# Where the denominators of the first four heads stand in TensorE's program

## The chip, the cores and the metric

The kernel runs on one core of a Trainium2 chip. The metric is the device time of one execution in microseconds, lower is better. In the profile PE is TensorE's matmuls, PEld its weight loads, DVE is VectorE, ACT is ScalarE, POOL is GpSimd and SP is SyncE.

## The reference

The input is 32 sequences of 256 tokens with 256 features. First come four recurrent (sLSTM) layers with their feed-forward parts, then, per sequence, an attention over a context and a quantised feed-forward layer. The change lies in the attention:

```python
q, k, v = (heads(q), heads(k), heads(v))          # 16 heads of 64 features
sim = jnp.einsum('bhid,bhjd->bhij', q, k) * SCALE
sim = jnp.where(mask[:, None, None, :], sim, max_neg)
sim = jnp.clip(sim, -5.0, 5.0)
attn = jax.nn.softmax(sim, axis=-1)
out = jnp.einsum('bhij,bhjd->bhid', attn, v)
```

Since the scores are clipped to -5 and 5, no maximum is taken off ahead of the exponential. The kernel multiplies the exponentials with the values, and separately with ones, which gives the denominators; the quotient is taken behind both.

## The kernel before, in words

The program has two stages, one after the other. The first holds the recurrent layers (lines up to 585). The second, `attend_and_feed` from line 586, has a loop over the batch of B = 32 sequences, written out by hand for each engine: each engine has its own queue in a fixed order, and semaphores tie them together. Batch j holds the projections and the attention of sequence j, woven with the feed-forward part of sequence j - 1 and the layer norms of sequence j + 2.

The attention of a batch goes in four quads q of four heads each. For quad q:

- `scores(j, pair)` on TensorE (line 857) forms the scores of two heads. It writes them to two of three PSUM banks (SCORES = 3), so a pair waits until VectorE has clipped the older heads in these banks: `clip_done` of 2 * pair - 1 heads.
- `clip(j, i)` on VectorE (line 1175) clips and masks the scores of head i into the SBUF tile `scores`, a ring of eight heads.
- `exps(j, i)` on ScalarE (line 1027) takes the exponential in place.
- `add_halves(j, i)` on POOL (line 771) adds the two halves (128 keys each) of the exponentials of head i, into the tile `exps_of_both_halves`. Behind the add of head 3 POOL splits the context of sequence j + 2 into a high and a low f16 part (`context_split`, lines 757 and 759), and behind the adds of heads 7, 11 and 15 it forms the low part of the attended values of the quad before (line 775).
- `attend(j, q, 0)` and `attend(j, q, 1)` on TensorE (line 867) multiply the exponentials of four heads with the first and the second half of their value features. The first waits for the exponentials of all four heads and for `ot_done`, the product of the quad before.
- `denominators(j, q)` on TensorE (line 879) multiplies the added halves of four heads with ones. It waits for `halves_added` of all four heads.
- `denominators(j, q)` on ScalarE (lines 1071 and 1073) takes the logarithm of the denominators, and the exponential of its negative. In ScalarE's order it stands between the exponentials of heads 4q + 5 and 4q + 6.
- `attended(j, q)` on VectorE (line 1260) multiplies the attended values with the inverse denominators.
- `out_project` on TensorE (line 911) projects the result.

VectorE's order around quad 0 of batch j, for 0 < j < 30: clips of heads 4 and 5; the rounding down of the first token tile of the hidden values (`h_round_down(f, 0)`, line 1231); clips of heads 6 and 7; `attended(j, 0)`; the rounding up of the second tile (`h_round_up(f, 1)`, line 1227, a multiplication and an addition over 128x1024 f32 from SBUF to SBUF); clips of heads 8 and 9; the low part of the next inputs (line 1322); the rounding down of the second tile (line 1231).

TensorE's order in a batch: the projections, and the first four score heads; then per quad what stands in the loop below. `x1_features` (line 902) turns the next batch's normed inputs, `transpose_h` and `feed_out` belong to the feed-forward part.

```python
for q in range(QUADS):
    if q + 1 < QUADS:
        scores(j, 2 * q + 2)
    if q == 0 and j + 1 < B:
        x1_features(j + 1)
    attend(j, q, 0)
    if q + 1 < QUADS:
        scores(j, 2 * q + 3)
    denominators(j, q)
    attend(j, q, 1)
```

Of the kernel before, what the change touches and what calls it, by code (L numbers as in the profile page):

```python
# [585 lines left out]
def attend_and_feed(nc, ctx, a, x4, out, kept):  # L586
# [128 lines left out]
    with nc.Block() as block:  # L715
# [91 lines left out]
        def _(pe):  # L807
# [39 lines left out]
            def scores(j, pair):  # L847

                if pair == 0:
                    pe.wait_ge(lo_done, SPLIT * (j + 1))  # L850
                else:
                    pe.wait_ge(clip_done, AHEADS * j + 2 * pair - 1)
                for kt in range(KT):
                    for part, (k_, q_) in enumerate(((k_hi, q_hi), (k_lo, q_hi), (k_hi, q_lo))):
                        for hh in range(2):
                            r = slice(ADH * hh, ADH * (hh + 1))
                            mm = nc.tensor.matmul(bank[:, (2 * pair + hh) % SCORES, kt * S:(kt + 1) * S],  # L857
                                                  k_[r, pair, kt * P:(kt + 1) * P], q_[r, pair, :], start=part == 0, stop=part == 2)
                            if kt == KT - 1 and part == 2:
                                mm.then_inc(s_ready, 1)  # L860

            def quad(j, q, stationary, b, at, done):

                for kt in range(KT):
                    for g in range(4):
                        i = 4 * q + g
                        mm = nc.tensor.matmul(bank[32 * g:32 * g + 32, b, at:at + S], stationary(kt, i),  # L867
                                              pr[:, i % RING, kt * S:(kt + 1) * S], start=kt == 0, stop=kt == KT - 1,
                                              skip_group_check=True)
                if done is not None:  # L870
                    mm.then_inc(done, 1)

            def denominators(j, q):
                n = QUADS * j + q
                pe.wait_ge(halves_added, 4 * (n + 1))
                if n > 0:
                    pe.wait_ge(den_step, 2 * n - 1)
                for g in range(4):
                    mm = nc.tensor.matmul(bank[32 * g:32 * g + 32, DEN, 0:S], ones32[:], psum[:, (4 * q + g) % RING, :], start=True,  # L879
                                          stop=True, skip_group_check=True)  # L880
                mm.then_inc(den_ready, 1)

            def attend(j, q, half):
                n = QUADS * j + q
                if half == 0:
                    pe.wait_ge(exp_done, 4 * (n + 1))
                    if q == 0:
                        pe.wait_ge(v_done, QUARTERS * (j + 1))
                    if n > 0:
                        pe.wait_ge(ot_done, n)  # L890
                quad(j, q, lambda kt, i: v[:, kt, i, 32 * half:32 * half + 32], AV, half * S, av_done if half else None)
# [4 lines left out]
            def x1_features(n):  # L896
                pe.wait_ge(x1_step, X1_OPS * (n + 1))
                if n > 1:
                    pe.wait_ge(h_done, ROUNDS * (n - 1))
                for h in range(HALF):  # L900
                    for tt in range(QT):
                        mm = nc.tensor.transpose(bank[:, FFB, h * S + tt * P:h * S + (tt + 1) * P], x1[:, tt, h * P:(h + 1) * P], identf[:])  # L902
                mm.then_inc(x1_turned, 1)
# [13 lines left out]
            def transpose_x(j, tt):  # L917
                pe.wait_ge(quant_step, x_quantised(j, tt))
                for h in range(HALF):
                    mm = nc.tensor.transpose(bank[:, OUTB, :].bitcast(BF16)[:, tt * D + h * P:tt * D + (h + 1) * P],  # L920
                                             xq[:, tt, h * P:(h + 1) * P], identb[:])
                mm.then_inc(xqt_ready, 1)

            def feed_in(j, r):

                tt, c = r // 2, r % 2
                if c == 0:
                    pe.wait_ge(xqt_done, QT * j + tt + 1)
                if r == 0 and j == 0:
                    pe.wait_ge(ff_ready, 1)  # L930
                if r == 0 and j > 0:
                    pe.wait_ge(z_done, QT * j)
                for m, read in enumerate((gate_done, h_done)):
                    if r > 0:
                        pe.wait_ge(read, ROUNDS * j + r)
                    w_ = ff_t[:, m, :].rearrange("p (h n) -> p h n", h=HALF)
                    for h in range(HALF):
                        mm = nc.tensor.matmul(bank[:, FFB + m, :], xqt[:, tt, h, :], w_[:, h, c * 512:(c + 1) * 512],  # L938
                                              start=h == 0, stop=h == HALF - 1)
                mm.then_inc(gu_ready, 1)  # L940

            def transpose_h(j):
                for tt in range(QT):
                    pe.wait_ge(hquant_step, h_quantised(j, tt))
                    if tt == 0 and j + 2 < B:
                        pe.wait_ge(x1_split, j + 3)
                    for c in range(FF // P):
                        mm = nc.tensor.transpose(bank[:, FFB + tt, :].bitcast(BF16)[:, c * P:(c + 1) * P],  # L948
                                                 hq[:, tt, c * P:(c + 1) * P], identb[:])
                    mm.then_inc(hqt_ready, 1)  # L950

            def feed_out(j):
                for tt in range(QT):
                    pe.wait_ge(hqt_done, QT * j + tt + 1)
                    w_ = ff_t[:, 2, :].rearrange("p (c n) -> p c n", c=FF // P)
                    for c in range(FF // P):
                        mm = nc.tensor.matmul(bank[:, FFB + tt, 0:D], hqt[:, tt, c, :], w_[:, c, :], start=c == 0,  # L957
                                              stop=c == FF // P - 1)
                    mm.then_inc(down_ready, 1)

            def first_units():
                for u in range(QUARTERS):
                    unit(0, u)
                for u in range(SPLIT, UNITS):
                    unit(0, u)
                pe.wait_ge(ident_ready, 2)
                x1_features(0)
                for u in range(QUARTERS, SPLIT):
                    unit(0, u)
                scores(0, 0)  # L970
                pe.wait_ge(ff_parts, 3)
                nc.tensor.matmul(bank[:, FFB + 1, 0:3], onesf[:], ff_part[:], start=True, stop=True).then_inc(ff_sums, 1)
                scores(0, 1)

            pe.wait_ge(consts, 1)
            for j in range(B):
                f = j - 1
                if j == 0:
                    first_units()
                else:  # L980
                    for u in range(UBANKS):
                        unit(j, u)
                    transpose_x(f, 0)
                    unit(j, UBANKS)
                    feed_in(f, 0)
                    transpose_x(f, 1)
                    for r in range(1, ROUNDS):
                        unit(j, UBANKS + r)
                        feed_in(f, r)
                    scores(j, 0)  # L990
                    unit(j, SPLIT + 1)
                    scores(j, 1)
                    unit(j, SPLIT + 2)
                    unit(j, SPLIT + 3)
# [3 lines that stand above are left out]
                    if q == 0 and j + 1 < B:  # L998
                        x1_features(j + 1)
                    attend(j, q, 0)  # L1000
                    if q + 1 < QUADS:
                        scores(j, 2 * q + 3)
                    denominators(j, q)
                    attend(j, q, 1)
                    if q == 2 and j > 0:
                        transpose_h(f)
                    if q == 3 and j > 0:
                        feed_out(f)
                    if q > 0:
                        out_project(j, 2 * q - 2)  # L1010
                        out_project(j, 2 * q - 1)
                out_project(j, APAIRS - 2)
                out_project(j, APAIRS - 1)
# [519 lines left out]
```

## Time and profile before

| what | value |
|---|---|
| median of 3 runs | 3733.89 us (3730.02 to 3734.52) |
| the profiled execution | 3732.63 us |
| its span | 3730.9 us |
| TensorE matmul busy | 3615.0 us, 97% |
| VectorE busy | 3460.5 us, 93% |
| ScalarE busy | 3064.7 us, 82% |
| GpSimd busy | 2253.7 us, 60% |
| granted TensorE clock, mean | 0.99 |
| batches of the second stage | from about 2262 us on |

The span is what the profiler saw between the first and the last instruction. A row of the timeline gives the start in microseconds from the span's start, the time taken, the engine, the line of the kernel, the instruction, what it writes and reads with its shape, and how many instructions the row merges; square brackets give the idle time of the engine ahead of it and who ended it. Matmuls are pipelined: a matmul's own duration is longer than its distance to the next one, so blocks on TensorE are compared by their starts. Of the other engines too, an instruction's time reaches a little over the start of the next one.

### The profile page before, as it was taken

The numbers are of one execution on the slowest core, as the hardware profiler recorded it, in microseconds if no ns is written. First come the engines' busy times: TensorE is split into PE (matmuls) and PEld (weight loads), VectorE is DVE, ScalarE is ACT, GpSimd is POOL, SyncE is SP. The second block draws the span as 40 slices with busy tenths as digits, with TensorE's granted clock in tenths as the row PEclk, the third lists the DMA queues.
The fourth block names the chain that finished last, engine by engine and source line by source line (L and its number), as shares of the span: only waits on it lengthen the run. The fifth ranks groups of instructions, "written<-read, shape, count | busy, mean of one in ns | idle before, by whom it ended". The sixth has DMA issues, their size and how long they took to land. (4 is left out here: it accounts for less than half of the span.)

```text
span 3730.9 us, 167466 instructions
## 1 busy us (share of the span) xinstructions
PE 3615.0 (97%) x71481; PEld 2282.1 (61%) x71481; DVE 3460.5 (93%) x9241; ACT 3064.7 (82%) x6357; POOL 2253.7 (60%) x2395
## 2 busy tenths in 40 slices
PE   6999999999999999999999987999999999999997
PEld 3666666665666666666666654666666666666664
DVE  8999999999999999999999987889988898888886
ACT  4999999999999999999999984677776677777675
POOL 3777777777777777777777764444444444444442
PEclk9999999999999999999999998999999999999998
DMA  2000221000000000000000000000000000100000
GB/s 82 25 25 25 56 59 53 25 25 25 25 25 25 25 25 25 25 25 25 25 25 25 25 26 18 24 24 24 24 24 24 24 24 28 32 24 24 24 16 10
DMA packets 99973, 104.27 MB, mean 28 GB/s; under 512 B 17297, under 2 KB 95005, under 8 KB 98729
## 3 DMA queue, kind: packets, MB, share of 16 engines
q1 hardware_dynamic: 99224, 93.56, 8.7%
q8 instruction: 560, 9.18, 1.0%
q14 instruction: 189, 1.54, 0.1%
HBM read 48.52 MB, written 17.53 MB: 18 GB/s over the span
## 5 line engine op out<-in xcount | busy, mean ns | idle before, releaser
L565 POOL TENSOR_TENSOR conv_products<-normed_features,conv_taps_by_token 128x256 f32<-128x256 f32 (+1 forms) x837 | 757.9, 919 | 530.2 <-ACT normed_features L348 530.1
L771 POOL TENSOR_TENSOR exps_of_both_halves<-scores 128x256 f32<-128x256 f32 x512 | 424.2, 851 | 583.8 <-ACT scores L1027 578.4
L295 PE MATMUL banks<-up_centred,after_cell_features 128*32 128x336 f32 x8928 | 740.3, 449 | 1.1 <-ACT after_cell_features L348 0.5
L295 PEld LDWEIGHTS banks<-up_centred,after_cell_features 128*32 128x32 f32 x8928 | 260.5, 109 | 277.6 <-issue 224.1
L302 PE MATMUL banks<-down,hidden_features 112*32 112x256 f32 x6696 | 419.2, 383 | 0.0
L578 POOL TENSOR_TENSOR conv_partial_sums<-conv_products,conv_partial_sums 128x512 f32<-128x512 f32 x279 | 370.5, 1328 | 21.9
L1027 ACT ACTIVATE scores<-scores 128x512 f32<-128x512 f32 x512 | 305.4, 626 | 77.7 <-DVE scores L1175 74.0
L366 ACT ACT_TABLE_LOAD x279 | 358.0, 1283 | 5.2
L381 ACT ACT_TABLE_LOAD x279 | 358.0, 1283 | 5.1
L1175 DVE SCALAR_TENSOR_TENSOR scores<-banks,score_top 128x512 f32<-128x512 f32 x512 | 327.9, 681 | 26.1 <-PE banks L857 25.5
L269 PE MATMUL banks<-recurrent_weights,h_features 64*32 64x256 f32 x8928 | 313.1, 379 | 0.3 <-DVE h_features L509 0.2
L867 PE MATMUL banks<-scores,v_tokens 128*32 128x256 f32 x4096 | 274.0, 385 | 11.9 <-ACT scores L1027 11.7
L579 POOL TENSOR_TENSOR conv_partial_sums<-conv_products,conv_partial_sums 128x256 f32<-128x256 f32 x279 | 265.1, 950 | 0.0
L302 PEld LDWEIGHTS banks<-down,hidden_features 112*32 112x32 f32 x6696 | 189.0, 109 | 121.3
L571 POOL TENSOR_TENSOR conv_partial_sums<-conv_products,conv_partial_sums 128x256 f32<-128x256 f32 x279 | 220.3, 790 | 65.9 <-DVEq L466 44.0
L835 PE MATMUL banks<-batch_inputs_hi,qkv_weights_hi 128*128 128x256 f16 x1024 | 196.0, 273 | 11.3 <-POOL batch_inputs_lo L759 9.8
L269 PEld LDWEIGHTS banks<-recurrent_weights,h_features 64*32 64x32 f32 x8928 | 196.1, 106 | 8.3 <-DVE h_features L509 1.5
L835 PE MATMUL banks<-batch_inputs_lo,qkv_weights_hi 128*128 128x256 f16 x1024 | 196.0, 273 | 0.0
L835 PE MATMUL banks<-batch_inputs_hi,qkv_weights_lo 128*128 128x256 f16 x1024 | 195.9, 273 | 0.0
L867 PEld LDWEIGHTS banks<-scores,v_tokens 128*32 128x32 f32 x4096 | 120.9, 110 | 107.6 <-ACT scores L1027 27.1
L269 PE MATMUL banks<-gate_weights,convolved_features 64*32 64x128 f32 x8928 | 186.2, 275 | 0.0
L503 DVE SCALAR_TENSOR_TENSOR convolved_features<-tanh_half_conv,conv_partial_sums 128x256 f32<-128x256 f32 x279 | 180.0, 645 | 0.5 <-ACT tanh_half_conv L365 0.5
(222 smaller groups left out, 9933.3 us busy)
## 6 DMA issues: line engine op xcount, KB each, us to landing
layer_inputs<-layer_outputs SPq DMA_DIRECT2D x279, 96.0 KB, 2.0
layer_inputs<-in_x SPq DMA_DIRECT2D x280, 32.0 KB, 1.8
x_scratch<-layer_outputs SPq DMA_DIRECT2D x279, 32.0 KB
x_tokens<-in_x SPq DMA_DIRECT2D x32, 256.0 KB, 3.0
context_features<-in_ctx SPq DMA_DIRECT2D x32, 256.0 KB, 3.7
layers_out<-x_scratch SPq DMA_DIRECT2D x32, 256.0 KB, 2.8
out<-result SPq DMA_DIRECT2D x64, 128.0 KB, 1.8
up_centred<-in_ff_up SPq DMA_DIRECT2D x1, 2688.0 KB
```

The lines of the kernel that those rows point to most:

```text
L269: mm = nc.tensor.matmul(bank[group(l), 2 * (j % 2) + odd, at + g0 * DH:at + g1 * DH], src[r, n, group(l)], w[r, l, n, g0:g1, :].rearrange( ...
L295: mm = nc.tensor.matmul(bank[group(l), b, 0:UP], xmt[:, n, group(l)], up[:, l, n, at:at + UP], start=n == 0, stop=n == HALF - 1, skip_grou ...
L302: mm = nc.tensor.matmul(bank[group(l), FD, 0:D], hidt[:, i, group(l)], down[:, l, i, :], start=i == 0, stop=i == UTILES - 1, skip_group_ch ...
L366: nc.scalar.preload_act_table_set(LOG_EXP)
L381: nc.scalar.preload_act_table(ACT.Gelu)
L565: return nc.gpsimd.tensor_tensor(prod[:, i:i + n], xnt[:, j % NRING].rearrange("p n t -> p (n t)")[:, None, :].broadcast_to([P, n, HALF * ...
L578: nc.gpsimd.tensor_tensor(new[:, 0:2], prod[:, 0:2], old[:, 1:3], ALU.add).then_inc(conv_done, 1)
L771: nc.gpsimd.tensor_tensor(psum[:, i % RING, :], pr[:, i % RING, 0:S], pr[:, i % RING, S:2 * S], ALU.add).then_inc(halves_added, 1)
L835: mm = nc.tensor.matmul(bank[:, b, i * S:(i + 1) * S], w_[:, m, h, (2 * n + i) * P:(2 * n + i + 1) * P], x_[:, j % SLOTS, src, h, :], star ...
L867: mm = nc.tensor.matmul(bank[32 * g:32 * g + 32, b, at:at + S], stationary(kt, i), pr[:, i % RING, kt * S:(kt + 1) * S], start=kt == 0, st ...
L1027: nc.scalar.activation(pr[:, i % RING, :], pr[:, i % RING, :], ACT.Exp, scale=S_SCALE).then_inc(exp_done, 1)
L1175: nc.vector.scalar_tensor_tensor(out=pr[:, i % RING, :].rearrange("p (k s) -> p k s", k=KT), in0=bank[:, i % SCORES, :].rearrange("p (k s) ...
```

## The change

In quad 0, TensorE's denominators move from behind the scores of heads 6 and 7 to in front of them, directly behind the first half of the product with the values. Quads 1 to 3 keep their order, and the other engines' programs are the same.

```diff
@@ -998,9 +998,12 @@
                     if q == 0 and j + 1 < B:
                         x1_features(j + 1)
                     attend(j, q, 0)
+                    if q == 0:
+                        denominators(j, q)
                     if q + 1 < QUADS:
                         scores(j, 2 * q + 3)
-                    denominators(j, q)
+                    if q > 0:
+                        denominators(j, q)
                     attend(j, q, 1)
                     if q == 2 and j > 0:
                         transpose_h(f)
```

## Rows read from the trace of the kernel before

**Rows 1.** Windows of batch 5 and batch 28: us, busy time by engine, clock, DMA.

```profile
2510.15:2554.93 44.78, 44.25 (x482) 29.04 (x482) 40.21 (x86) 31.46 (x60) 20.07 (x22) 1.00 0.08 26
3540.44:3585.82 45.38, 44.31 (x482) 29.03 (x482) 40.82 (x86) 31.47 (x60) 19.97 (x22) 1.00 0.08 25
```

**Rows 2.** Timeline of batch 5, TensorE's matmuls (first rows of blocks, some merged).

```profile
2511.50 1.07 PE L867 MATMUL banks<-scores,v_tokens 128*32 128x256 f32 x16
2512.51 0.28 PE L857 MATMUL banks<-q_hi,k_hi 64*128 64x256 f16 x2
...
2513.26 0.64 PE L879 MATMUL banks<-exps_of_both_halves,ones_for_sums 128*32 128x256 f32 x8
2513.72 1.05 PE L867 MATMUL banks<-scores,v_tokens 128*32 128x256 f32 x16
...
2515.89 1.07 PE L867 MATMUL banks<-scores,v_tokens 128*32 128x256 f32 x16 [0.37 <-ACT scores L1027]
2516.90 0.28 PE L857 MATMUL banks<-q_hi,k_hi 64*128 64x256 f16 x2
...
2522.51 0.28 PE L857 MATMUL banks<-q_hi,k_hi 64*128 64x256 f16 x2 [0.17 <-DVE scores L1175]
...
2527.01 0.42 PE L867 MATMUL banks<-scores,v_tokens 128*32 128x256 f32 x4
...
2527.89 0.40 PE L879 MATMUL banks<-exps_of_both_halves,ones_for_sums 128*32 128x256 f32 x4
```

**Rows 3.** Timeline of batch 5, VectorE.

```profile
2513.37 1.29 DVE L1175 SCALAR_TENSOR_TENSOR scores<-banks,score_top 128x512 f32<-128x512 f32 x2 [0.17 <-PE banks L857]
2514.89 0.69 DVE L1260 TENSOR_TENSOR attended<-banks,denominator_log 128x512 f32<-128x512 f32 x1 [0.23 <-ACT denominator_log L1073]
2515.50 0.74 DVE L1227 TENSOR_SCALAR gate<-hidden_f,quant_scale 128x1024 f32<-128x1024 f32 x1
2516.16 0.68 DVE L1175 SCALAR_TENSOR_TENSOR scores<-banks,score_top 128x512 f32<-128x512 f32 x1
...
2517.36 0.68 DVE L1322 TENSOR_TENSOR batch_inputs_lo<-banks,batch_inputs_hi 128x512 f16<-128x512 f32 x1
```

**Rows 4.** Timeline of batch 5, POOL: adds of heads 2-3, 4-7, and 6 alone.

```profile
2510.16 1.95 POOL L771 TENSOR_TENSOR exps_of_both_halves<-scores 128x256 f32<-128x256 f32 x2 [0.83 <-ACT scores L1027]
...
2514.19 3.33 POOL L771 TENSOR_TENSOR exps_of_both_halves<-scores 128x256 f32<-128x256 f32 x4
...
2515.57 1.27 POOL L771 TENSOR_TENSOR exps_of_both_halves<-scores 128x256 f32<-128x256 f32 x1
```

**Rows 5.** Timeline of batch 5, ScalarE.

```profile
2514.39 0.42 ACT L1073 ACTIVATE denominator_log<-denominator_log 128x256 f32<-128x256 f32 x1
2514.71 1.13 ACT L1027 ACTIVATE scores<-scores 128x512 f32<-128x512 f32 x2
```

**Rows 6.** Timeline of batch 28 (four rows), then of batch 30 (two).

```profile
3545.78 1.35 DVE L1227 TENSOR_SCALAR gate<-hidden_f,quant_scale 128x1024 f32<-128x1024 f32 x1
3545.84 0.74 POOL L771 TENSOR_TENSOR exps_of_both_halves<-scores 128x256 f32<-128x256 f32 x1
3547.05 0.68 DVE L1175 SCALAR_TENSOR_TENSOR scores<-banks,score_top 128x512 f32<-128x512 f32 x1
3547.79 0.28 PE L857 MATMUL banks<-q_hi,k_hi 64*128 64x256 f16 x2 [0.54 <-DVE scores L1175]
...
3635.84 0.72 POOL L771 TENSOR_TENSOR exps_of_both_halves<-scores 128x256 f32<-128x256 f32 x1 [1.22 <-ACT scores L1027]
3635.94 1.18 DVE L1227 TENSOR_SCALAR gate<-hidden_f,quant_scale 128x1024 f32<-128x1024 f32 x1
```

**Rows 7.** A wait of TensorE, whole span; line 1227's group from 2331 us on.

```profile
PE banks L879 <- POOL exps_of_both_halves L771: 9.6, 2, 5.1
...
L1227 DVE TENSOR_SCALAR gate<-hidden_f,quant_scale 128x1024 f32<-128x1024 f32 x64 | 49.4, 772 | 0.0
```

## The prediction, made before the changed kernel ran

> **What bounds the kernel now.** The two token-recurrent parts of the program are one after the other; only the second (32 batches of attention and feed-forward) is touched. Read first the windows: a batch takes 44.78 us, of which TensorE is busy 44.25 [rows 1]. It is the bound, so the change can only act through gaps between its blocks. The timeline of TensorE in batch 5 shows where they are [rows 2]. I name the blocks by heads and read starts: values 0a (first half of the product with the values, heads 0 to 3) 2511.50, scores 6-7 2512.51, denominators 0 2513.26, values 0b 2513.72, (scores 8-9), values 1a 2515.89, scores 10-11 2516.90, scores 14-15 2522.51. Two carry a wait: values 1a (0.37, for ScalarE's exps) and scores 14-15 (0.17, for VectorE's clips). Scores 10-11 shows none, and yet it too is tied to VectorE: the clip of head 8, which it needs, ends at 2516.16 + 0.68 = 2516.84 [rows 3], and it starts 0.06 later. From the product 2514.89 on VectorE runs back to back: 0.69 long with the next start 0.61 later, rounding 0.74 with the next 0.66 later, two clips in 1.20 [rows 3]. So TensorE and VectorE are both full here, and VectorE's position after 2514.89 is TensorE's position at scores 10-11 and 14-15.
>
> **The change, part by part.** It issues the same instructions; one block of eight matmul records per batch moves in front of another block, on TensorE's queue alone. No DMA, nothing of SP, POOL, ACT or VectorE is reordered.
>
> *TensorE's own time.* Values 0a to scores 6-7 takes 1.01, scores 6-7 to denominators 0.75, denominators to values 0.46 [rows 2]. In the new order the first step is values to denominators, which quad 3 has already: 2527.01 to 2527.89, 0.88 [rows 2]. Denominators to scores has no row; the same block before values takes 0.46, and scores behind values cost 1.01 - 0.88 = 0.13 more than denominators do. Lower bound 0.43 (no such cost), upper 0.59; I take 0.56, nearest to the switch that rows show. Sum before 1.01 + 0.75 + 0.46 = 2.22, after 0.88 + 0.56 + 0.75 = 2.19. Nothing to win or lose: values 0b starts at about 2513.70.
>
> *The wait that moves.* The block waits until POOL has added the two halves of the exps of heads 0 to 3. Behind it now stand scores 6-7. The last of these adds ends 2510.16 + 1.95 = 2512.11 [rows 4]; denominators would start at 2511.50 + 0.88 = 2512.38. Covered with 0.27 to spare; in batch 0 too, where TensorE's long waits for POOL (9.6 in two [rows 7]) belong to later quads. If the cover failed by 0.3, scores 6-7 would come that much later; see below why even this would hardly cost more.
>
> *What comes earlier.* Exp of the denominator's log starts 2513.26 + 1.13 = 2514.39 and ends 2514.81 [rows 5], and the product `attended(0)` at 2514.89 waited 0.23 for it [rows 3]. Now it ends at 2512.38 + 1.13 + 0.42 = 2513.93 and waits for nobody. ScalarE's exps of heads 6 and 7 lie right behind it (2514.71, 1.13 for two [rows 5]); freed, they follow the clips.
>
> *What comes later.* Scores 6-7 start at 2512.38 + 0.56 = 2512.94, 0.43 later (0.30 to 0.46 by the bounds). Their clips start 0.43 later, 2513.80 instead of 2513.37, and end the pair at 2515.09; exps of 6 and 7 end near 2515.75, where before it was 2515.84. Values 1a, which waits for them and for `attended(0)`, comes 0.1 earlier or stands. But `attended(0)` is queued behind the clips: 2513.80 + 1.20 = 2515.00, 0.11 later than before. The first round of the reckoning is thus +0.11 on VectorE, and by the first part +0.11 per batch on TensorE, 31 x 0.11 = 3.4 us.
>
> *What this 0.11 meets.* The rounding behind it (line 1227, 128x1024 f32) would start at 2515.00 + 0.61 = 2515.61. POOL adds heads 4 to 7 back to back from 2514.19 (3.33 for four, started by the end of its context split, which the change doesn't touch), and the add of head 6 starts at 2515.57 [rows 4]. Before, the rounding started 0.07 ahead of it (2515.50), took 0.74, and the add took 1.27 instead of about 0.72: POOL waited for VectorE. In batch 28 it went the other way [rows 6]: rounding 3545.78, add 3545.84, 0.06 apart; the add took 0.74 and the rounding 1.35. The next clip came at 3547.05, 1.21 after the add's start; scores 10-11 carry a wait of 0.54, and the batch took 45.38, 0.60 more [rows 1]. Likewise batch 30, where the add began first (3635.84 before 3635.94) and the rounding took 1.18 [rows 6]. All 64 roundings take 49.4 [rows 7]; 61 x 0.75 + 1.35 + 2 x 1.18 = 49.5, so these three (the last in batch 31) are the only stalled ones. The kernel before wins this race in 28 of the batches 1 to 29, by a hair.
>
> After the change the rounding comes 0.04 behind the add, 0.10 too late to win, in every batch. The clip of head 8 then starts at 2515.57 + 1.21 = 2516.78 instead of 2516.16, and all that follows on both engines 0.62 later, as batch 28 shows. The start of the rounding itself drops out of this: anywhere between 2515.51 and 2516.1 it ends the same, so the error of my 0.56, or a short wait for POOL, cost nothing.
>
> The Trainium skill, SBUF — State Buffer, section "Who interferes with whom", says that VectorE in a 2-port mode and GpSimd hold the shared port pair exclusively, for the whole instruction, whoever is first. The direction agrees with the rows. By its "whole instruction" the rounding would wait to the add's end, 2515.57 + 0.74, and the clip start near 2516.97: 0.81 per batch and 22 us in all, where batch 28 shows less; the sum goes by the row.
>
> *Sum.* 28 batches x 0.62 = 17.4. Batch 28 has its stall already. Batches 30 and 31 have no context split, POOL is idle, and the add of head 6 follows its exp, now about 0.2 earlier; the stalled rounding ends that much earlier: 2 x -0.2. Batch 0 is held by POOL anyway: 0. Together +17.0 us on the profiled execution's 3732.63 (span 3730.9), 3749.6; on the median 3733.89, which is 1.26 above it, 3750.9.
>
> **The rivals.**
> *A, VectorE is not later (not slower).* If scores behind denominators cost so little that scores 6-7 move by less than 0.32, `attended(0)` stays at 2514.89 or before, and the rounding keeps its win. The lower bound 0.43 for the block gives 0.30, so it is just possible; against it stands that every step to scores in these rows costs a switch. Then 0 to -1 us: 3733 to 3734. It decides at a shift of 0.32. Chance 0.08.
> *B, later but still first.* POOL's add of head 6 begins 0.1 or more later than I read, since the clips now lie otherwise against POOL's split. Then only the 0.11: +3.4, 3737.3. For it: POOL's starts are rough; against: the split and the adds have the same starts in batches whatever ran on VectorE beside them. Chance 0.12.
> *C, a second meeting.* The rounding down of the same tile, or the centring in quad 2, loses another half microsecond to an add, in every batch: 28 x 0.5 more, 3765. Batch 28 went without it. Chance 0.07.
> That the order doesn't change is excluded: it is written out by hand on one queue.
>
> **How the numbers follow.** Forecast 0.73. About 0.2% (7.5 us) is what a measurement of this kernel can tell from no change. Slower by more: forecast and C, some of B's spread, less a little of the forecast's: 0.78. Within: A and B, 0.19. Faster by more needs 0.24 per batch, more than any wait that the new order frees: 0.03. The forecast's own range is 3746 to 3755; to hold 8 in 10 it reaches down to B: 3736 to 3757.
>
> **What the profile would show.** Right: batches of 45.4 us; line 1227 (128x1024) at 1.2 to 1.35 us in about half its 64 instances, their sum near 66 us; POOL's third add of quad 1 at 0.74 instead of 1.27; scores 10-11 with a wait of some 0.5 for VectorE; the exp of the denominator's log 1.0 earlier in the batch; no wait of denominators 0 for POOL. Wrong: batches of 44.8 to 44.9 with roundings of 0.75 (A or B), or denominators 0 waiting for POOL, or a shift of scores 6-7 outside 0.30 to 0.46.

## The result and the profile after

| | before | after |
|---|---|---|
| median | 3733.82 us (5 runs, 3730.02 to 3734.52) | 3748.44 us (5 runs, 3747.07 to 3750.43) |
| span of the profiled execution | 3730.9 us | 3746.7 us |

The ratio is 1.0042, 95% interval 1.0027 to 1.0056: slower by 14.6 us.

The windows of the changed kernel: batch 5, and the stretch from the start of batch 1 to the start of batch 30 (columns as in [rows 1]).

```profile
2511.50:2556.88 45.38, 44.26 (x482) 29.12 (x482) 40.64 (x86) 31.69 (x60) 19.98 (x23) 1.00 0.08 25
2329.96:3646.41 1316.45, 1283.38 (x13893) 844.29 (x13922) 1178.70 (x2466) 918.89 (x1712) 579.80 (x639) 1.00 0.08 24
```

And the kernel before over the same 29 batches:

```profile
2331.03:3630.59 1299.56, 1283.03 (x13921) 842.17 (x13920) 1166.92 (x2466) 912.33 (x1712) 581.94 (x638) 1.00 0.08 25
```

A batch takes 45.38 instead of 44.78 us [rows 1], and 29 batches 16.9 more. TensorE is busy for the same time, so the loss is idle time of TensorE. VectorE's busy time grew by 11.8 though its instructions are the same in number (2466): some of them last longer. What stands ahead of batch 1 was 1.1 shorter in this execution (it begins at 2329.96 instead of 2331.03), and what follows the start of batch 30 took 100.3 in both, which is why the span differs by 15.8.

The timeline of batch 5 of the changed kernel, TensorE, from values 0a on, the other score rows left out; it answers to [rows 2]:

```profile
2512.84 1.07 PE L867 MATMUL banks<-scores,v_tokens 128*32 128x256 f32 x16
2513.73 0.61 PE L879 MATMUL banks<-exps_of_both_halves,ones_for_sums 128*32 128x256 f32 x8
2514.28 0.28 PE L857 MATMUL banks<-q_hi,k_hi 64*128 64x256 f16 x2
...
2515.04 1.07 PE L867 MATMUL banks<-scores,v_tokens 128*32 128x256 f32 x16
2516.04 0.28 PE L857 MATMUL banks<-q_hi,k_hi 64*128 64x256 f16 x2
...
2517.18 1.07 PE L867 MATMUL banks<-scores,v_tokens 128*32 128x256 f32 x16 [0.30 <-ACT scores L1030]
2518.85 0.28 PE L857 MATMUL banks<-q_hi,k_hi 64*128 64x256 f16 x2 [0.60 <-DVE scores L1178]
...
2524.45 0.28 PE L857 MATMUL banks<-q_hi,k_hi 64*128 64x256 f16 x2 [0.16 <-DVE scores L1178]
```

VectorE, POOL and ScalarE of the same batch, which answer to [rows 3], [rows 4] and [rows 5]:

```profile
2515.14 1.29 DVE L1178 SCALAR_TENSOR_TENSOR scores<-banks,score_top 128x512 f32<-128x512 f32 x2 [0.59 <-PE banks L857]
2516.35 0.68 DVE L1263 TENSOR_TENSOR attended<-banks,denominator_log 128x512 f32<-128x512 f32 x1
2516.95 1.25 DVE L1230 TENSOR_SCALAR gate<-hidden_f,quant_scale 128x1024 f32<-128x1024 f32 x1
2518.11 0.68 DVE L1178 SCALAR_TENSOR_TENSOR scores<-banks,score_top 128x512 f32<-128x512 f32 x1
...
2515.53 3.24 POOL L771 TENSOR_TENSOR exps_of_both_halves<-scores 128x256 f32<-128x256 f32 x4
...
2516.92 0.72 POOL L771 TENSOR_TENSOR exps_of_both_halves<-scores 128x256 f32<-128x256 f32 x1
...
2514.83 0.42 ACT L1076 ACTIVATE denominator_log<-denominator_log 128x256 f32<-128x256 f32 x1
2515.87 1.23 ACT L1030 ACTIVATE scores<-scores 128x512 f32<-128x512 f32 x2 [0.62 <-DVE scores L1178]
```

Batch 5 starts at 2511.50 here and at 2510.15 before, so 1.35 is to be taken off for a comparison. See the pair in the middle: POOL's add of head 6 starts at 2516.92 and takes 0.72, the rounding on VectorE starts at 2516.95 and takes 1.25. Before, the rounding was 0.07 ahead and took 0.74, and the add took 1.27. The two have changed roles, and scores 10-11 (2518.85) wait 0.60 for the clip behind the rounding. Of such a pair the text says below that one wins (it takes its usual time) and the other loses (it takes about 0.5 more).

### The profile page after: what moved, and what is told of

The parts are those of the page before. It is cut to its first block and busy times, and to the rows that moved or that the text cites. A ratio compares the mean times of both kernels' runs of the same rounds, so it can differ in the third digit from the quotient of the medians.

```text
span 3746.7 us, 167434 instructions
## 1 busy us (share of the span) xinstructions
PE 3616.7 (97%) x71449; PEld 2284.6 (61%) x71481; DVE 3471.2 (93%) x9241; ACT 3071.7 (82%) x6357; POOL 2251.2 (60%) x2395
```

## Experiments

Two theories were tested. The race: the extra time comes from the rounding of 128x1024 on VectorE losing to POOL's add of head 6, and the moved denominators only shift VectorE by the 0.1 us that decides it. The rival: the lateness of scores 6-7 and of what hangs on them costs the time by itself. Each ratio below is to runs of the kernel before from the same set, whose median was 3734.09 us for e1 to e4 and 3733.92 for e5 to e7.

### e1: the new order, POOL later by 0.14 us

The memset does nothing for the result; it pushes POOL's adds back.

```diff
+    spare = sb("spare", [P, P])
...
                     if i == 3 and j + 2 < B:
                         context_split(j + 2)
+                        nc.gpsimd.memset(spare[:], 0.0)
```

> The changed kernel, with a memset of 128x128 f32 into a spare tile on POOL behind each context split (30 batches), so that POOL's adds of heads 4 to 7 start later by about 0.2 us. Theory of the race: the rounding (128x1024, first started 0.04 us behind the add of head 6) is again ahead of it, takes 0.75 to 0.8 instead of 1.25, the add takes 1.2 to 1.27, scores 10-11 come 0.45 to 0.5 earlier in the batch; a batch takes 44.9 to 45.0 instead of 45.38, the kernel 3735 to 3740. Rival, lateness of scores 6-7 alone (what POOL does beside it is no matter): batches stay at 45.38 and the time at 3748. More work on POOL must then give the same or a longer time.

Measured: 3735.18 us, ratio to the kernel before 1.0003 (0.9994 to 1.0012). Windows of batch 5, then VectorE, POOL and TensorE at the race:

```profile
2514.60:2559.50 44.90, 44.26 (x482) 29.13 (x482) 40.14 (x86) 31.66 (x60) 20.20 (x24) 1.00 0.08 26
...
2520.05 0.74 DVE L1232 TENSOR_SCALAR gate<-hidden_f,quant_scale 128x1024 f32<-128x1024 f32 x1
...
2520.15 1.23 POOL L772 TENSOR_TENSOR exps_of_both_halves<-scores 128x256 f32<-128x256 f32 x1
...
2521.45 0.28 PE L859 MATMUL banks<-q_hi,k_hi 64*128 64x256 f16 x2
```

With 30 more instructions on POOL and TensorE's order that of the changed kernel, 13 of the 14.6 us are gone. The rounding starts 5.45 behind the batch's start as in the changed kernel, but now 0.10 ahead of the add, and takes 0.74. In all 29 batches the rounding wins. What remains, 0.12 per batch, is the part of the rival: VectorE reaches the rounding 0.10 later than before (5.45 instead of 5.35 behind the batch's start).

### e2: the old order, VectorE later by less than 0.1 us

```diff
                         if s_ == 1:
+                            nc.vector.memset(spare[:, 0:1], 0.0)
                             h_round_up(f, 1)
```

> The kernel before, with a memset of 128x1 f32 into a spare tile on VectorE between attended(j, 0) and the rounding up of the second tile. TensorE's order is the old one. Theory of the race: the rounding starts some 0.05 to 0.1 us later, behind POOL's add of head 6, and takes 1.2 to 1.3; the next clip starts 1.21 behind the add's start as in batch 28; a batch takes 45.38 and the kernel 3748 to 3751, although only 0.1 us of work is added. Rival, without a race: 44.78 + 0.1, 3734 to 3737.

Measured: 3748.19 us, ratio 1.0033 (1.002 to 1.0046), the time of the changed kernel, with TensorE's program untouched. VectorE, then POOL, in batch 5:

```profile
2517.35 1.33 DVE L1228 TENSOR_SCALAR gate<-hidden_f,quant_scale 128x1024 f32<-128x1024 f32 x1
2517.38 0.06 DVE L1441 MEMSET spare<- 128x1 f32 x1
2518.60 0.68 DVE L1176 SCALAR_TENSOR_TENSOR scores<-banks,score_top 128x512 f32<-128x512 f32 x1
...
2517.41 0.72 POOL L772 TENSOR_TENSOR exps_of_both_halves<-scores 128x256 f32<-128x256 f32 x1
```

An instruction of 0.06 us moved the rounding from 0.07 ahead of the add to 0.06 ahead, and the batch takes 45.37 (2330.48 to 3646.46 for 29 of them). This is the whole change of time without the change. The profile draws the memset inside the rounding, though it stands ahead of it in VectorE's queue, so the recorded start of the rounding is too early here, and starts that lie this close are not exact.

### e3: the old order, POOL later

The control of e1: its POOL memset in the kernel before.

> The kernel before with POOL's memset of the first run, as a control of it. Theory of the race: the rounding starts 2515.50 as before in batch 5, now inside POOL's add of head 5, whose hold ends about 0.55 us behind its start; it waits 0.1 to 0.2, is still ahead of the add of head 6, and batches take 44.8 to 45.0: 3734 to 3740. If more work on POOL sped kernels up by itself, this one would be faster than 3733.

Measured: 3735.3 us, ratio 0.9999 (0.999 to 1.0009); a batch takes 44.84. The memset doesn't speed a kernel up by itself; it cost 0.06 per batch here, since the rounding (2516.97, 0.80) now starts inside POOL's add of head 5 and waits 0.06 for it, less than the 0.1 to 0.2 expected.

### e4: the old order, the second rounding down before x1_lo

The race has a second case in each batch: the rounding down of the same tile (line 1231) took 1.23 in batch 5, behind POOL's `attended_lo`, and never less than 1.13. Here it is put where it arrives first.

```diff
-                    if s_ == 2 and j + 1 < B:
-                        x1_lo(j + 1)
...
                         if s_ == 2:
                             h_round_down(f, 1)
+                    if s_ == 2 and j + 1 < B:
+                        x1_lo(j + 1)
```

> The kernel before, with the rounding down of the second tile (line 1231, 128x1024) in front of the low part of the next inputs (x1_lo) on VectorE in quad 1, instead of behind it. Theory: it starts at 2517.36, at the end of POOL's add of head 7 and 0.1 ahead of POOL's attended_lo, wins, and takes 0.7 to 0.8 instead of 1.23; VectorE is 0.5 earlier, the wait of scores 14-15 for its clips (0.27 by starts) goes, but attended_lo is held up to about 2519.2 and the output projection starts 0.15 later. A batch 44.65, the kernel 3729 to 3731. Rival: attended_lo wins, the rounding takes 1.3 or more at the earlier place; no gain, 3733 to 3740.

Measured: 3727.97 us, ratio 0.9981 (0.9972 to 0.999): faster than both kernels. Windows of batch 5, VectorE, POOL and TensorE there:

```profile
2510.66:2555.27 44.61, 44.19 (x480) 29.03 (x481) 39.95 (x86) 31.57 (x60) 20.08 (x22) 1.00 0.08 26
...
2517.87 0.72 DVE L1231 TENSOR_SCALAR hidden_quant<-gate 128x1024 bf16<-128x1024 f32 x1
...
2517.99 1.62 POOL L775 TENSOR_TENSOR attended_lo<-attended,attended_hi 128x512 f16<-128x512 f32 x1
...
2522.85 0.28 PE L857 MATMUL banks<-q_hi,k_hi 64*128 64x256 f16 x2
```

The rounding down starts 0.12 ahead of `attended_lo` and wins; POOL's 1.16 become 1.62, which delays the output projection by 0.07 where 0.15 was expected; so the batch came out at 44.61, a little below the 44.65 written, and the kernel below the 3729 to 3731 expected. Scores 14-15, which carried a wait before [rows 2], carry none. In two of the 29 batches, 22 and 29, the first race was lost all the same: the rounding up took 1.34, and batch 22 took 45.28. The last section shows the rows.

### e5: the new order, POOL later by a hair

As e1, with `spare[:, 0:1]` in the memset.

> The changed kernel with a memset of 128x1 f32 on POOL behind each context split, where the first run had 128x128. POOL's adds of heads 4 to 7 start 0.03 to 0.07 later, the add of head 6 at 5.45 to 5.49 behind the batch's start, against 5.45 for the rounding: still not 0.06 behind it. Theory of the race: the rounding still loses, and its end, tied to the add's start, comes later by the same 0.03 to 0.07; batches 45.41 to 45.45, the kernel 3749 to 3751, the same as the changed kernel or slower, while 0.15 more of delay made it 13 us faster. Rival, that any later POOL helps in proportion (a quarter of the first run's 0.49 per batch): 45.25, 3745.

Measured: 3749.84 us, ratio 1.0041 (1.0026 to 1.0056). VectorE and POOL in batch 5:

```profile
2518.36 1.27 DVE L1232 TENSOR_SCALAR gate<-hidden_f,quant_scale 128x1024 f32<-128x1024 f32 x1
2519.55 0.68 DVE L1180 SCALAR_TENSOR_TENSOR scores<-banks,score_top 128x512 f32<-128x512 f32 x1
...
2518.35 0.72 POOL L772 TENSOR_TENSOR exps_of_both_halves<-scores 128x256 f32<-128x256 f32 x1
```

Even with the add only 0.01 ahead by the profile's starts, the rounding loses; its end moves with the add's start, the next clip 1.20 behind it, and a batch takes 0.02 more (29 take 1317.08), just below the 45.41 expected. A delay of 0.02 on POOL costs a little, 0.14 gives back 13 us: a step, not a slope. (In batch 1 of this execution the rounding lost with a start 0.01 ahead.)

### e6: the new order with both races won

e1 and e4 together.

> The changed kernel, POOL later by the 128x128 memset, and the rounding down of the second tile in front of x1_lo, the two edits that each took a lost race away. Theory: both roundings win (0.75 and 0.72), VectorE is 0.5 earlier at the clip of head 10 than in the first run (9.08 to 8.55), scores 14-15 wait for nobody; attended_lo ends later, output projection at 9.1. Batches 44.70 to 44.75, the kernel 3731 to 3733, 2 to 4 us above the kernel before with the roundings swapped (44.60, 3728), which is what is left of the denominators' move: scores 10-11 0.1 later. Rival, that the move helps once no race is lost (values 1a starts 0.06 earlier): at or below 44.60, 3728 or less.

Measured: 3729.09 us, ratio 0.9987 (0.9977 to 0.9996), below the 3731 expected in absolute terms; a batch took 44.70 as expected, and e4's 44.61. e6 loses neither race in any of the 29 batches, e4 loses both in batches 22 and 29. Where neither is lost, the kernel with the new order of the denominators is 0.1 per batch slower. Over all 29 batches (1296.50 against 1294.87) only 1.6 is left of the 3.0 or so that this makes, since e4 pays about 0.67 in each of its two lost batches. e6 also has the memset on POOL that e4 has not; that the 0.1 comes from the move is read from VectorE, which reaches the rounding 5.45 instead of 5.35 behind the batch's start, and wasn't tested apart from the memset. The medians of e6 and e4, from separate sets of runs, are too near to say more.

### e7: the new order, only the rounding down moved

> The changed kernel with the rounding down of the second tile in front of x1_lo, POOL untouched. The first rounding loses as before (1.25). The second starts at 7.82, inside POOL's attended_lo (7.24 on, held for about 1.03), waits for its end at 8.27 and takes about 1.1 to 1.15 instead of 1.22. Theory of the race: the place of an instruction alone gives nothing; VectorE gains 0.1, batches 45.28 to 45.35, the kernel 3745 to 3748. Rival, that the swap is worth its 0.17 per batch (6 us) in any kernel: 45.21, 3742.

Measured: 3745.69 us, ratio 1.0029 (1.0019 to 1.0039); a batch takes 45.28. VectorE and POOL in batch 5:

```profile
2521.49 1.13 DVE L1234 TENSOR_SCALAR hidden_quant<-gate 128x1024 bf16<-128x1024 f32 x1
...
2520.92 1.15 POOL L775 TENSOR_TENSOR attended_lo<-attended,attended_hi 128x512 f16<-128x512 f32 x1
```

The same edit as e4, but the instruction arrives 0.57 behind `attended_lo` and waits. In the changed kernel it had lost to the next instruction on POOL, the add of head 8, which it followed by 0.06. It took VectorE 1.13 in place of 1.22, and gave 0.10 per batch where e4 gave 0.17. The place in the program did not matter, the meeting did.

| kernel | a batch, us | starts: rounding up less add of head 6 | rounding up, us | median, us |
|---|---|---|---|---|
| before | 44.78 | -0.07 | 0.74 | 3733.82 |
| after | 45.38 | +0.03 | 1.25 | 3748.44 |
| e1 after, POOL later | 44.90 | -0.10 | 0.74 | 3735.18 |
| e2 before, VectorE later | 45.37 | -0.06 | 1.33 | 3748.19 |
| e3 before, POOL later | 44.84 | -0.21 | 0.80 | 3735.3 |
| e4 before, down first | 44.61 | -0.07 | 0.74 | 3727.97 |
| e5 after, POOL a hair later | 45.40 | +0.01 | 1.27 | 3749.84 |
| e6 after, both | 44.70 | -0.12 | 0.74 | 3729.09 |
| e7 after, down first | 45.28 | +0.04 | 1.24 | 3745.69 |

## Why the prediction was right

It came out at 3748.44 against 3750.9, inside the range and on the forecast's own mechanism. Of the 2.5 that it is off, 0.5 is the price of a lost race (below). The rest lies elsewhere: the profiled execution is itself the median after, where before it was 1.3 under the median taken, and what stands ahead of batch 1 was 1.1 shorter; against these, 0.4 written for batches 30 and 31 was not gained.

**TensorE's own time.** Values to denominators was put at 0.88 and took 0.89 (2512.84 to 2513.73). Denominators to scores had no row and was taken as 0.56 between 0.43 and 0.59; it took 0.55. Values 0b start 3.54 behind the batch's start, where they stood at 3.57.

**The wait that moved.** No wait of the denominators' matmuls for POOL shows in batches 1 to 29, but the cover is thinner than the 0.27 written. The block begins with loading weights, at 2513.52, and the last add ends at 2512.72 + 0.73 = 2513.45, so 0.07 is left; the prediction compared with the start of the matmuls. In batch 31 the cover fails: the load waits 0.38 for POOL, and denominators start 0.97 behind the values instead of 0.89.

**What came earlier.** The exp of the denominator's log starts 3.33 behind the batch's start instead of 4.24, 0.9 earlier (1.0 was written), and `attended(0)` no longer waits for it. Values 1a come 0.06 earlier. None of this reaches the end of the batch, since scores 10-11 wait for VectorE.

**What came later.** Scores 6-7 by 0.43, their clips by 0.43, `attended(0)` by 0.11 (4.85 for 4.74), all as reckoned.

**The race.** The rounding was expected 0.04 behind the add and is 0.03 behind. Its price was a little off: 0.62 per batch was written and 0.60 measured, because the clip follows the add's start by 1.19 (2518.11 less 2516.92), where batch 28 had shown 1.21. The 0.60 could be read from [rows 1]: batch 28 took 45.38. The 0.62 adds batch 28's distance to the add's start of batch 5. Over 29 batches 16.9 were lost, of them 28 x 0.60 = 16.8 in the batches that had won before. In batches 30 and 31 the rounding takes 0.91 instead of 1.18, as expected, but the time does not follow: from the start of batch 30 to the end both kernels take 100.3, where 0.4 less was written. What took the gain up was not traced in full; the late denominators of batch 31 cost 0.08 of it at their place. The roundings' sum is 62.8 instead of the 66 written: a rounding that starts 0.1 later and ends at the same time lasts 1.25, not 1.35.

```profile
L1230 DVE TENSOR_SCALAR gate<-hidden_f,quant_scale 128x1024 f32<-128x1024 f32 x64 | 62.8, 981 | 0.0
```

**The rivals.** A needed a shift below 0.32; it was 0.43. B is what e1 made by hand: the shift without the loss costs 0.12 per batch and 3735.18 us, against 3737.3 written. Over 29 batches e1 takes 1302.23, 2.7 more than before, which is 28 x 0.12 less the 0.6 that batch 28 had lost. C did not come: behind the rounding everything keeps the distances of batch 28. The sentence on the Trainium skill (SBUF — State Buffer, "Who interferes with whom") can now be judged: that one of the two is stopped until the other is through agrees with the batches shown; that the rounding runs in a 2-port mode no trace shows. The stop seems shorter than the other's recorded time. In the changed kernel the rounding is longer by 1.25 - 0.74 = 0.51; if it needs its whole 0.74 once it is let go, it resumes 0.54 behind the add's start, whose record is 0.72 long. Whether the record outlasts the add, or a part of the 0.74 passes during the stop, no run here separates. The measured figure decides, and the 22 us reckoned from the page's wording and the recorded end would have been too much.

## What to carry to other kernels

Where two engines run back to back and some of their instructions exclude each other, the cost of moving anything ahead of them can lie less in the move than in the order in which these instructions meet. List the pairs by their starts, and look for a batch or an iteration in which the meeting fell the other way by chance: it carries the price of the change before the change is made. A lost meeting was mended here by letting the favoured side come a tenth of a microsecond ahead, by a change on either engine (e1, e4); on the side with slack even an idle instruction did it. Look at every batch and not at one: a head start of 0.06 or 0.07 was not safe.

## What was not expected of the hardware

The recorded starts don't tell the winner when the rounding is ahead by 0.05 to 0.08 us. The kernel before lost in batch 28 with the rounding 0.06 ahead of the add [rows 6], and won in batch 7 with the same 0.06. e4 lost in batch 22 with 0.06 by its rows, and won in batches around it with 0.07. The rounding, then the add, in batch 7 of the kernel before:

```profile
2605.05 0.74 DVE L1227 TENSOR_SCALAR gate<-hidden_f,quant_scale 128x1024 f32<-128x1024 f32 x1
2605.11 1.28 POOL L771 TENSOR_TENSOR exps_of_both_halves<-scores 128x256 f32<-128x256 f32 x1
```

And in batch 22 of e4:

```profile
3274.28 1.34 DVE L1227 TENSOR_SCALAR gate<-hidden_f,quant_scale 128x1024 f32<-128x1024 f32 x1
3274.34 0.72 POOL L771 TENSOR_TENSOR exps_of_both_halves<-scores 128x256 f32<-128x256 f32 x1
```

In e1 and e6 the rounding was at least 0.09 ahead in batches 1 to 29 and won all 58 times; where the add was ahead, it won every time. In between the kernel before won 28 of 29, e4 27 of 29, and e2, whose recorded starts are too early, none of 29. What decides in between is not shown: it may be that the claim is laid a little behind the recorded start, but this was not tested by itself.

And a memset that does nothing for the result can take 13 us away (e1) or add 14 (e2). The memsets of e2 last 31 x 0.06 = 1.8 us together; the time grew by eight times that.
